# Turning undivided exponentials in the last attention stage, with two order tables made anew

## The chip, the cores and the metric

The kernel runs on one core of one Trainium2 chip. The metric is the device time of one execution, in microseconds. The core has five instruction streams, each executed in order: TensorE (PE; its weight loads are shown as PEld), VectorE (DVE), ScalarE (ACT), GpSimd (POOL) and SyncE (SP), which here only issues DMAs. They meet at semaphores alone.

## The reference

Four transformer blocks follow each other on x (batch 8, 128 tokens, width 256), with a context of the same shape.

```python
x = L0(x, ctx)   # 16 heads of 16: cross-attention to ctx, key mask; MLP 256-1024-256
x = L1(x, ctx)   # x attends to [ctx, x]; RMS norm; MLP
x = L2(x, ctx)   # twice: 16 heads of 128, cross-attention to ctx; MLP ("M2")
x = L3(x, ctx)   # "L3s" self-attention, "L3c" cross-attention, 16 heads of 16; MLP

# L3's attention
scores = einsum('bhqd,bhkd->bhqk', q, k) / sqrt(HD)
scores = scores * mask - 10000.0 * (1.0 - mask)
probs  = softmax(scores, axis=-1)
ctx    = einsum('bhqk,bhkd->bhqd', probs, v)     # v = ln_out @ w_v + b_v
x      = x + ctx @ w_o + b_o
```

## The kernel before

The program has three stages. **Stage A** (`ORDER_ONE`: L0 and L1) and **stage C** (`ORDER_TWO`: the MLP of L2, then L3s, L3c and their MLP) are lists of steps, one list for each engine, written out by hand: each engine runs its own steps in its list's order, and the semaphores make each step wait for what it reads and for the PSUM bank that it overwrites. A step's last number on PE is its PSUM bank. Between them stage B (the two attentions of L2) is a loop over 16 turns. The batch is cut into four streams `k` of two batch elements `b`.

In stage C attention runs in 16 **units** `n`, one for each layer (L3s, L3c), stream and batch element. A unit has 16 heads of 128 x 128 scores and is worked in two halves `r` of eight heads; half-unit `u = 2n + r` lives in `tiles[u % 4]` (128 x 1024 floats), so two units are under way at most. The steps of a unit, with the lines of the profile:

- `scores n`: PE multiplies into banks 0 to 3 (L842); DVE multiplies by the mask into the tile (L1191); POOL subtracts from the mask's offset (L1828).
- `minima n`: DVE takes each row's minimum (L1201); ACT takes the exponentials, head by head (`exp n r`, L1593).
- `even n r`: DVE sums the rows (L1206) and takes reciprocals (L1208); POOL multiplies the whole tile by them (L1834).
- `turn n r`: PE transposes the tile in two halves of four heads into banks 4 and 5 (L852), ACT copies them to `PT` (L1559).
- `weigh n`: PE multiplies `PT` with the values into bank 6 (L867); ACT adds the value bias and writes `OT` (L1508, `HEADS_ON["C"] = "ACT"`).
- `project n`: PE multiplies `OT` with the output weights (L881), DVE adds it and the pre-biased residual `xb` to x (L1222). POOL makes `xb` in `residual` (L1811).

The rest of stage C's lists are layer norms (DVE statistics, POOL `rstd` at L1747, ACT `xn`, PE transposes L717), projections (L730, L738, L794) and the MLPs (`up` L810, `down` L826).

Of the kernel before, what the change touches and what calls it, by code (L numbers as in the profile page):

```python
# [501 lines left out]
class Drains:  # L502
# [17 lines left out]
    ctx 0 0, turn_in L0 in 0 5, ctx 1 0, q L0 0 3, k L0 0 0 2, ctx 2 7, k L0 1 0 4, scores 0, k L0 2 0 7, ctx 3 5, v L0 2 0 4, scores 1,  # L520
    turn_in L0 in 3 5, v L0 3 0 7, turn_in L0 in 1 2, v L0 0 0 1, q L0 3 3, q L0 1 0, turn 0 0, scores 2, turn 0 1, turn_in L0 in 2 7, turn 1 0, weigh 0,
    scores 3, q L0 2 7, turn 1 1, k L0 3 0 1, project 0 4, weigh 1, v L0 1 0 3, turn 2 0, project 1 7, scores 4, turn 2 1, k L1 0 0 7, weigh 2, turn 3 0,
    turn_in L0 mlp 0 7, scores 5, turn 3 1, project 2 7, weigh 3, v L1 0 0 0, up L0 0 0 1, project 3 0, up L0 0 2 2, up L0 0 4 3, up L0 0 6 7, turn 4 0,
    scores 6, turn 4 1, down L0 0 0 7, down L0 0 1 0, turn_in L0 mlp 1 3, turn 5 0, weigh 4, scores 7, turn 5 1, project 4 7, turn_in L1 in 0 0, weigh 5,
    up L0 1 0 1, up L0 1 2 4, k L1 0 1 3, project 5 2, up L0 1 4 0, turn 6 0, q L1 0 1, up L0 1 6 7, scores 8, turn 6 1, k L1 1 0 7, down L0 1 0 1,
    turn_in L0 mlp 2 0, down L0 1 1 7, turn 7 0, turn_in L1 in 1 7, weigh 6, scores 9, turn 7 1, k L1 1 1 7, project 6 1, weigh 7, turn 8 0, v L1 0 1 7,
    scores 10, turn 8 1, project 7 7, v L1 1 0 0, q L1 1 1, up L0 2 0 3, up L0 2 2 2, up L0 2 4 7, turn 9 0, weigh 8, scores 11, turn 9 1, up L0 2 6 7,
    turn 10 0, weigh 9, down L0 2 0 7, scores 12, turn 10 1, k L1 2 0 7, turn 11 0, weigh 10, scores 13, turn 11 1, project 9 7, turn_in L0 mlp 3 4,
    weigh 11, down L0 2 1 3, v L1 1 1 2, up L0 3 0 4, up L0 3 2 7, project 11 2, turn 12 0, turn_in L1 in 2 7, turn 12 1, scores 14, weigh 12, turn 13 0,
    up L0 3 4 1, up L0 3 6 4, scores 15, turn 13 1, q L1 2 7, k L1 2 1 0, down L0 3 0 4, weigh 13, scores 16, turn 14 0, v L1 2 0 7, turn 14 1,  # L530
    down L0 3 1 1, v L1 2 1 2, project 13 5, turn_in L1 mlp 0 0, turn_in L1 in 3 2, turn 15 0, weigh 14, scores 17, turn 15 1, k L1 3 0 7, turn 16 0,
    weigh 15, scores 18, turn 16 1, up L1 0 0 7, project 15 0, up L1 0 2 3, up L1 0 4 1, up L1 0 6 2, turn 17 0, weigh 16, scores 19, turn 17 1,
    v L1 3 0 7, turn_in L1 mlp 1 0, k L1 3 1 3, down L1 0 0 1, q L1 3 2, turn 18 0, weigh 17, scores 20, turn 18 1, v L1 3 1 7, weigh 18, turn 19 0,
    scores 21, turn 19 1, down L1 0 1 7, project 17 0, up L1 1 0 1, up L1 1 2 2, up L1 1 4 7, turn 20 0, weigh 19, scores 22, turn 20 1, up L1 1 6 7,
    project 19 1, turn 21 0, weigh 20, scores 23, turn 21 1, down L1 1 0 7, turn_in L1 mlp 2 1, down L1 1 1 3, weigh 21, turn 22 0, up L1 2 0 0,
    turn 22 1, up L1 2 2 1, turn 23 0, weigh 22, up L1 2 4 7, turn 23 1, up L1 2 6 0, weigh 23, project 21 4, project 23 7, down L1 2 0 1, keys_of 0,
    turn_in L1 mlp 3 7, down L1 2 1 5, up L1 3 0 2, up L1 3 2 5, up L1 3 4 7, up L1 3 6 0, turn_in L1 out 1 4, turn_in L1 out 0 2, down L1 3 0 5,
    down L1 3 1 7, turn_in L1 out 2 3, keys_of 1, values_of 0, turn_in L1 out 3 7, queries_of 0, values_of 1, values_of 2,
    values_of 3, queries_of 1
""",  # L540
    "ACT": """
    wcut L0 k, ctx 0 0, turn_in L0 in 0 5, ctx 1 0, k L0 0 0 2, ctx 2 7, k L0 1 0 4, k L0 2 0 7, ctx 3 5, exp 0 0, exp 0 1, v L0 2 0 4, turn_in L0 in 3 5,
    v L0 3 0 7, turn_in L0 in 1 2, v L0 0 0 1, exp 1 0, turn 0 0, exp 1 1, turn 0 1, turn_in L0 in 2 7, exp 2 0, turn 1 0, exp 2 1, turn 1 1, k L0 3 0 1,
    exp 3 0, v L0 1 0 3, turn 2 0, exp 3 1, turn 2 1, k L1 0 0 7, turn 3 0, exp 4 0, turn 3 1, turn_in L0 mlp 0 7, exp 4 1, v L1 0 0 0, exp 5 0,
    up L0 0 0 1, up L0 0 2 2, up L0 0 4 3, turn 4 0, up L0 0 6 7, turn 4 1, exp 5 1, exp 6 0, exp 6 1, turn 5 0, turn_in L0 mlp 1 3, turn 5 1,
    turn_in L1 in 0 0, exp 7 0, up L0 1 0 1, up L0 1 2 4, k L1 0 1 3, up L0 1 4 0, turn 6 0, up L0 1 6 7, exp 7 1, k L1 1 0 7, exp 8 0, turn 6 1, exp 8 1,
    turn_in L0 mlp 2 0, turn_in L1 in 1 7, turn 7 0, turn 7 1, k L1 1 1 7, exp 9 0, turn 8 0, v L1 0 1 7, turn 8 1, exp 9 1, v L1 1 0 0, exp 10 0,
    exp 10 1, up L0 2 0 3, up L0 2 2 2, turn 9 0, up L0 2 4 7, turn 9 1, up L0 2 6 7, exp 11 0, exp 11 1, turn 10 0, turn 10 1, k L1 2 0 7, turn 11 0,
    turn 11 1, exp 12 0, exp 12 1, turn_in L0 mlp 3 4, exp 13 0, exp 13 1, v L1 1 1 2, up L0 3 0 4, up L0 3 2 7, turn 12 0, turn_in L1 in 2 7, turn 12 1,
    turn 13 0, up L0 3 4 1, up L0 3 6 4, exp 14 0, turn 13 1, exp 14 1, k L1 2 1 0, exp 15 0, exp 15 1, turn 14 0, v L1 2 0 7, turn 14 1, exp 16 0,  # L550
# [1711 lines left out]
```

## Time and profile before

| | us |
|---|---|
| median of 3 runs | 1029.7 |
| the 3 runs | 1029.73, 1029.70, 1028.91 |
| the profiled execution | 1029.54 |
| its span | 1028.3 |
| PE busy in the span | 997.2 |
| DVE, ACT, POOL busy | 789.0, 586.1, 712.5 |

The span runs from the first to the last recorded instruction; 1.24 us of the profiled execution lie around it. Busy time is the union of an engine's instructions. A matmul's record reaches from its start to the end of its drain, and so overlaps the next one's: in a stream of them the distance between starts, not the mean duration, is what one costs. Stage C begins at about 780 us. The granted TensorE clock stands as PEclk, 1.00 for 2.4 GHz.

### The profile page before, as it was taken

To read this page: it belongs to the slowest core of one execution; us is meant where nothing else is said; L and a number is where in the kernel's file an instruction comes from. 1 tells how busy PE (TensorE), PEld (TensorE's weight loads), DVE (VectorE), ACT (ScalarE), POOL (GpSimd) and SP (SyncE) were. 2 spreads that over 40 slices of the span, in tenths; PEclk is the share of its full clock that TensorE was granted. 3 is DMA by queue.
4 is the path that set the end of the run, shared out by engine and by line. 5 is a ranking of instruction groups with operands and counts; after the bars stand their busy time and mean duration, and the time that the engine had idled before them with its cause. 6 is when DMAs were issued, how large, how long until landed. Compare 5 with 4: busy or idle time off the path is not lost.

```text
span 1028.3 us, 21233 instructions
## 1 busy us (share of the span) xinstructions
PE 997.2 (97%) x8212; PEld 897.7 (87%) x8212; DVE 789.0 (77%) x1272; ACT 586.1 (57%) x1305; POOL 712.5 (69%) x659
## 2 busy tenths in 40 slices
PE   7899999999999999999999999999998999998998
PEld 7788878888889999999998999999997988777877
DVE  7997888998357778988868878888875488898761
ACT  5998888797535323233233333232335589999982
POOL 6895476755578888556368987756647488999961
PEclk9999999999999999999999999999999999999999
DMA  8200001000121220211120111110130000000000
GB/s 335 116 2 2 1 2 42 2 1 2 47 77 33 74 62 30 62 42 42 42 86 21 42 42 42 31 43 23 44 141 1 1 2 2 2 1 2 12 11 21
DMA packets 34219, 40.72 MB, mean 40 GB/s; under 512 B 2159, under 2 KB 31305, under 8 KB 32713
## 3 DMA queue, kind: packets, MB, share of 16 engines
q1 hardware_dynamic: 34121, 39.38, 11.6%
q8 instruction: 66, 1.08, 0.4%
q14 instruction: 32, 0.26, 0.1%
HBM read 38.32 MB, written 1.05 MB: 38 GB/s over the span
## 4 chain that ended last, share of the span: by engine, by line
PE 76%; POOL 11%; DVE 6%; ACT 4%; issue 2%; DMA 0%; SPq 0%; DVEq 0%; POOLq 0%; ACTq 0%
PE psum L946 10%; PE psum L810 9%; PE psum L826 9%; PE psum L964 7%; PE psum L1012 7%; PE psum L852 5%; PE psum L999 5%; PE psum L978 5%; PE psum L931 4%; PE psum L738 3%; PE psum L842 3%; PE psum L867 3%; PE psum L988 2%; POOL C tile L1828 2%; PE psum L881 2%
## 5 line engine op out<-in xcount | busy, mean ns | idle before, releaser
L1983 POOL TENSOR_TENSOR B tile<-B tile,B rec 128x1024 f32<-128x1024 f32 x32 | 61.0, 1912 | 101.9 <-DVE B rec L1369 101.9
L1834 POOL TENSOR_TENSOR A tile<-A tile,outer rec 128x1024 f32<-128x1024 f32 x48 | 91.0, 1905 | 57.8 <-DVE outer rec L1208 57.7
L1685 ACT COPY B PT<-psum 128x512 f32<-128x512 f32 x64 | 33.0, 600 | 138.0 <-PE psum L988 138.0
L1593 ACT ACTIVATE A tile<-A tile,outer min 128x128 f32<-128x128 f32 (+1 forms) x256 | 92.3, 448 | 2.6 <-DVE outer min L1201 2.5
L1593 ACT ACTIVATE C tile<-C tile,outer min 128x128 f32<-128x128 f32 x256 | 77.8, 401 | 1.1 <-DVE outer min L1201 1.0
L964 PE MATMUL psum<-B v hi,cT hi 128*128 128x256 f32 x256 | 71.9, 281 | 0.3 <-ACT B kT L1508 0.3
L964 PE MATMUL psum<-B v hi,cT lo 128*128 128x256 f32 x256 | 71.7, 280 | 0.0
L964 PE MATMUL psum<-B v lo,cT hi 128*128 128x256 f32 x256 | 71.7, 280 | 0.0
L1834 POOL TENSOR_TENSOR C tile<-C tile,outer rec 128x1024 f32<-128x1024 f32 x32 | 60.7, 1902 | 7.7 <-DVE outer rec L1208 7.7
L1194 DVE TENSOR_TENSOR A tile<-m,psum 128x1024 f32<-128x1024 f32 x48 | 56.5, 1216 | 9.1 <-PE psum L842 7.9
L1206 DVE TENSOR_REDUCE outer sum<-A tile 128x4 f32<-128x1024 f32 (+1 forms) x48 | 58.0, 1208 | 4.9 <-ACT A tile L1593 4.9
L1559 ACT COPY A PT<-psum 128x512 f32<-128x512 f32 x96 | 51.4, 590 | 18.1 <-PE psum L852 10.9
L999 PEld LDWEIGHTS psum<-B PT,B v 128*128 128x128 f32 x512 | 59.4, 192 | 1.1
L978 PE MATMUL psum<-B kT,B qT 128*128 128x128 f32 x512 | 59.8, 275 | 0.0
L999 PE MATMUL psum<-B PT,B v 128*128 128x128 f32 x512 | 59.8, 275 | 0.0
L978 PEld LDWEIGHTS psum<-B kT,B qT 128*128 128x128 f32 x512 | 58.5, 192 | 0.1
L826 PE MATMUL psum<-weights,C aT 128*128 128x256 f32 x256 | 57.2, 380 | 1.2 <-ACT C aT L1550 1.2
L826 PE MATMUL psum<-weights,A aT 128*128 128x256 f32 x256 | 57.8, 380 | 0.1
L852 PEld LDWEIGHTS psum<-ident,A tile 128*128 128x128 f32 x384 | 42.1, 141 | 18.2 <-issue 11.4
L1508 ACT ACTIVATE B OT0 hi<-psum,cols 128x512 fp32r<-128x512 f32 x32 | 21.9, 688 | 60.5 <-PE psum L999 60.4
L1201 DVE TENSOR_REDUCE outer min<-A tile 128x4 f32<-128x1024 f32 (+1 forms) x48 | 55.9, 1207 | 0.0
L826 PEld LDWEIGHTS psum<-weights,C aT 128*128 128x128 f32 x256 | 48.0, 190 | 7.8 <-issue 1.6
(358 smaller groups left out, 3550.6 us busy)
## 6 DMA issues: line engine op xcount, KB each, us to landing
raw<-in_wq SPq DMA_DIRECT2D x32, 128.0 KB, 2.9
raw<-in_wk SPq DMA_DIRECT2D x32, 128.0 KB, 3.0
raw<-in_wv SPq DMA_DIRECT2D x16, 256.0 KB, 2.8
raw<-in_wo SPq DMA_DIRECT2D x16, 256.0 KB, 2.7
weights<-in_weights_c SPq DMA_DIRECT2D x4, 1024.0 KB, 6.0
weights<-in_weights_a SPq DMA_DIRECT2D x1, 3072.0 KB, 21.5
weights<-in_weights_a SPq DMA_DIRECT2D x1, 2048.0 KB, 12.4
wide<-in_bias_v SPq DMA_DIRECT2D x2, 1024.0 KB, 10.1
```

The source lines that it names most:

```text
L810: i = pe.matmul(bank(z)[:, n * T:(n + 1) * T], w[wp][:, c, n * P:(n + 1) * P], h[hp][:, c, :], start=(c, wp, hp) == (0, 0, 0), stop=c == C ...
L826: i = pe.matmul(bank(z)[:, 0:D], part.aT(k)[:, c, b * P:(b + 1) * P], w2[:, c, :], start=c == 0, stop=c == FC - 1)
L852: i = pe.transpose(bank(4 + half)[:, j * P:(j + 1) * P], part.tiles[u % 4][:, q * P:(q + 1) * P], m.ident[:, :])
L946: i = pe.matmul(bank(z + n), m.block(kind, wt, wp), m.half_of(kind, src, sp), start=(wp, sp) == (0, 0), stop=wp == 1)
L964: i = pe.matmul(bank(z)[:, k * 2 * HK:(k + 1) * 2 * HK], m.bcT[cp][:, c, (2 * n + k) * S:(2 * n + k + 1) * S], m.cut["v"][wp][:, c, :], st ...
L978: i = pe.matmul(bank(z + b // 4)[:, (b % 4) * S:(b % 4 + 1) * S], m.qT[h][:, b * S:(b + 1) * S], m.kT[h][:, b * S:(b + 1) * S], start=True ...
L999: i = pe.matmul(bank(z)[:, k * P:(k + 1) * P], m.vv[:, 4 * n + k, h * HK:(h + 1) * HK], m.bPT[:, h, n, k * P:(k + 1) * P], start=True, sto ...
L1012: i = pe.matmul(bank(z)[:, k * D:(k + 1) * D], m.bOT[h][op][:, (2 * n + k) * S:(2 * n + k + 1) * S], m.cut["o"][wp][:, h, :], start=(h, op ...
L1206: dve.tensor_reduce(part.sum[:, u % 4, 0:ly.per], tile(u, ly.nk), AX.X, ALU.add).then_inc(s["sum_made"].sem, s["sum_made"].mark((st, u)))
L1593: i = act.activation(of_head, of_head, ACT.Exp, bias=part.min[:, u % 4, h:h + 1], scale=-1.0)
L1834: pool.tensor_tensor(tile(u, ly.nk), tile(u, ly.nk), part.rec[:, u % 4, 0:ly.per].unsqueeze(2).to_broadcast([P, ly.per, ly.nk]), ALU.mult) ...
L1983: pool.tensor_tensor(tv, tv, m.brec[:, h, :].unsqueeze(2).to_broadcast([P, B, S]), ALU.mult).then_inc(s["normalised"].sem, s["normalised"] ...
```

## The change

**Lists.** Both tables of steps are new for all four engines. Stage A's has the same steps in another order. Stage C's has one step more, `rows`, and `weigh` is added to the lists of engines that did not have it.

**Undivided exponentials (stage C only).** `turn` on PE no longer waits for `evened`, the division on POOL, but for `exp_made`. `even n r` on POOL no longer touches the 128 x 1024 tile: it spreads the 8 reciprocals of each row to 128 x 64 twice (each reciprocal repeated for the 16 columns of its head) into a new buffer `rec_rows`. At the end of `weigh n` PE waits for both of them and transposes `rec_rows` (two 128 x 128) into the second half of bank 6. ACT copies these 128 x 256 back to `rec_rows`, and DVE multiplies the weighed heads in bank 6 by them into `OT`, in one instruction, where ACT had written `OT` in two. The heads of stage C thus move from ACT to DVE.

**Bias.** Since the value bias is no longer added to the heads, the step `rows` multiplies it once with the output weights of L3s and L3c on PE, and DVE adds the two rows to the output biases; `residual` of L3's attentions waits for that.

```diff
-HEADS_ON = {"A": "DVE", "C": "ACT"}
+HEADS_ON = {"A": "DVE", "C": "DVE"}
...
+            self.Cs.rec_rows = sc("C rec rows", [P, 2, C, P])
...
         def turn(n, r):
-            pe.wait_ge(s["evened"].sem, s["evened"].at((st, u)))
+            ready = "exp_made" if st == "C" else "evened"
+            pe.wait_ge(s[ready].sem, s[ready].at((st, u)))
...
# weigh, PE, behind the 16 matmuls of the unit
+            if st == "C":
+                pe.wait_ge(s["evened"].sem, s["evened"].at((st, 2 * n + 1)))
+                for c in range(C):
+                    i = pe.transpose(bank(6)[:, (C + c) * P:(C + c + 1) * P], part.rec_rows[:, n % 2, c, :], m.ident[:, :])
+        def rows(z):
+            once("w_late_loaded", 32)
+            claim(z, "rows_made", "rows")
+            for n, name in enumerate(("L3s", "L3c")):
+                for c in range(C):
+                    i = pe.matmul(bank(z)[:, n * D:(n + 1) * D], layers[name].bv[:, c:c + 1].to_broadcast([P, P]), layers[name].wo[:, c, :],
+                                  start=c == 0, stop=c == C - 1)
...
# reciprocal, DVE
+            if st == "C" and n >= 2:
+                dve.wait_ge(s["evened"].sem, s["evened"].at((st, u - 4)))
# heads, DVE
+            if st == "C":
+                dve.wait_ge(s["rec_copied"].sem, s["rec_copied"].at(("C", n)))
+                dve.tensor_tensor(part.OT[b][:, :, :], bank(6)[:, 0:C * P].rearrange("p (c q) -> p c q", c=C), part.rec_rows[:, n % 2, :, :], ALU.mult).then_inc(
+                    s["heads_drained"].sem, s["heads_drained"].mark((ly.name, k, b)))
+                return
...
# weigh, ACT
+            elif what == "weigh" and st == "C":
+                act.wait_ge(s["weighed"].sem, s["weighed"].at((st, a[0])))
+                act.copy(part.rec_rows[:, a[0] % 2, :, :], bank(6)[:, C * P:2 * C * P].rearrange("p (c q) -> p c q", c=C)).then_inc(
+                    s["rec_copied"].sem, s["rec_copied"].mark((st, a[0])))
...
# even, POOL
+            if st == "C":
+                if n >= 2:
+                    pool.wait_ge(s["heads_drained"].sem, s["heads_drained"].at((units[n - 2][0].name, *units[n - 2][1:3])))
+                for c in range(C):
+                    i = pool.tensor_copy(part.rec_rows[:, n % 2, c, r * 4 * HD:(r + 1) * 4 * HD].rearrange("p (j q d) -> p j q d", j=2, q=2),
+                                         part.rec[:, u % 4, :].rearrange("p (j c q) -> p j c q", j=2, c=C)[:, :, c, :].unsqueeze(3).to_broadcast([P, 2, 2, HD]))
+                i.then_inc(s["evened"].sem, s["evened"].mark((st, u)))
+                return
...
# the lists, stage C, PE, the first line of each
-    output 0, output 1, output 2, turn_in M2 mlp 0 7, output 3, turn_in M2 mlp 1 1, up M2 0 0 4, up M2 0 2 5, up M2 0 4 1, up M2 0 6 2,
+    output 0, output 1, output 2, output 3, turn_in M2 mlp 0 4, rows 2, up M2 0 0 2, up M2 0 2 4, up M2 0 4 7, up M2 0 6 2, turn_in M2 mlp 1 1,
```

Three places of stage C show what moves. The first is POOL from the mask work of unit 6 (a row with `wide`, L3c's mask, x2) to that of unit 9; `outer rec` are the reciprocals. Before:

```order
L1828 TENSOR_TENSOR C tile<-wide,C tile 128x1024 x2
L1834 TENSOR_TENSOR C tile<-C tile,outer rec 128x1024
L1747 TENSOR_TENSOR outer rstd<-outer ve,half 128x2
L1828 TENSOR_TENSOR C tile<-wide,C tile 128x1024 x2
L1834 TENSOR_TENSOR C tile<-C tile,outer rec 128x1024
L1811 TENSOR_TENSOR raw<-x_all,rows 128x512
L1834 TENSOR_TENSOR C tile<-C tile,outer rec 128x1024 x2
L1828 TENSOR_TENSOR C tile<-wide,C tile 128x1024 x2
L1834 TENSOR_TENSOR C tile<-C tile,outer rec 128x1024
L1817 TENSOR_TENSOR C h lo<-C xn,C h hi 128x512
L1828 TENSOR_TENSOR C tile<-wide,C tile 128x1024 x2
L1834 TENSOR_TENSOR C tile<-C tile,outer rec 128x1024
```

and with the change, where `C rec rows` is the new buffer and `x2` or `x4` counts instructions, two to a half-unit:

```order
L1865 TENSOR_TENSOR C tile<-wide,C tile 128x1024 x2
L1875 COPY C rec rows<-outer rec 128x64 x4
L1865 TENSOR_TENSOR C tile<-wide,C tile 128x1024 x2
L1782 TENSOR_TENSOR outer rstd<-outer ve,half 128x2
L1848 TENSOR_TENSOR raw<-x_all,rows 128x512
L1875 COPY C rec rows<-outer rec 128x64 x4
L1865 TENSOR_TENSOR C tile<-wide,C tile 128x1024 x2
L1875 COPY C rec rows<-outer rec 128x64 x2
L1854 TENSOR_TENSOR C h lo<-C xn,C h hi 128x512
L1782 TENSOR_TENSOR outer rstd<-outer ve,half 128x2
L1875 COPY C rec rows<-outer rec 128x64 x2
L1865 TENSOR_TENSOR C tile<-wide,C tile 128x1024 x2
```

Each division of a 128 x 1024 tile between the pairs of mask work has become two copies of 128 x 64. The second place is PE from `weigh 4` on, behind the keys of L3c's stream 2 (`C tile` are the exponentials, `C PT` their turned copy). Before:

```order
L867 MATMUL psum<-C PT,C vaug 32x128 x16
L717 MATMUL psum<-ident,C xn 128x128 x4
L852 MATMUL psum<-ident,C tile 128x128 x8
L842 MATMUL psum<-C kT,C qT 128x256 x8
L852 MATMUL psum<-ident,C tile 128x128 x8
L881 MATMUL psum<-weights,C OT 128x256 x2
```

and with the change:

```order
L871 MATMUL psum<-C PT,C vaug 32x128 x16
L877 MATMUL psum<-ident,C rec rows 128x128 x2
L856 MATMUL psum<-ident,C tile 128x128 x16
L845 MATMUL psum<-C kT,C qT 128x256 x8
L871 MATMUL psum<-C PT,C vaug 32x128 x16
L877 MATMUL psum<-ident,C rec rows 128x128 x2
L856 MATMUL psum<-ident,C tile 128x128 x8
L720 MATMUL psum<-ident,C xn 128x128 x4
```

Each weighing is now followed by two transposes of `rec rows`, and `weigh 5` now comes right behind the scores of unit 7; behind the transposes stand the turns and scores of later units. The third place is DVE, from the last sum of unit 5 to those of unit 6 (`OT` are the heads). Before:

```order
L1206 TENSOR_REDUCE outer sum<-C tile 128x8
L1208 RECIPROCAL outer rec<-outer sum 128x8
L1201 TENSOR_REDUCE outer min<-C tile 128x8 x2
L1191 TENSOR_TENSOR C tile<-psum,wide 128x1024 x2
L1206 TENSOR_REDUCE outer sum<-C tile 128x8
L1208 RECIPROCAL outer rec<-outer sum 128x8
L1239 TENSOR_SCALAR outer nb<-outer mv,outer rstd 128x1 x2
L1222 TENSOR_TENSOR x_all<-psum,raw 128x256
L1201 TENSOR_REDUCE outer min<-C tile 128x8 x2
L1206 TENSOR_REDUCE outer sum<-C tile 128x8
```

and with the change, from the minima of unit 6 on:

```order
L1220 TENSOR_REDUCE outer min<-C tile 128x8 x2
L1236 TENSOR_TENSOR C OT<-psum,C rec rows 128x256
L1210 TENSOR_TENSOR C tile<-psum,wide 128x1024 x2
L1225 TENSOR_REDUCE outer sum<-C tile 128x8
L1229 RECIPROCAL outer rec<-outer sum 128x8
L1225 TENSOR_REDUCE outer sum<-C tile 128x8
L1229 RECIPROCAL outer rec<-outer sum 128x8
L1236 TENSOR_TENSOR C OT<-psum,C rec rows 128x256
L1220 TENSOR_REDUCE outer min<-C tile 128x8 x2
L1265 TENSOR_SCALAR outer nb<-outer mv,outer rstd 128x1 x2
L1248 TENSOR_TENSOR x_all<-psum,raw 128x256
```

The heads' multiplication is a new row between the minima of one unit and the masking of another; sums and reciprocals keep their number.

## Rows read from the trace of the kernel before

**Rows 1.** Busy shares of the whole span, from the page (40 slices).

```profile
PE 997.2 (97%) x8212; PEld 897.7 (87%) x8212; DVE 789.0 (77%) x1272; ACT 586.1 (57%) x1305; POOL 712.5 (69%) x659
...
PE   7899999999999999999999999999998999998998
```

**Rows 2.** Busy time by stage, from the windows (columns in the first row).

```profile
core 0: us, PE busy (x) PEld busy (x) DVE busy (x) ACT busy (x) POOL busy (x), PEclk, DMA share, GB/s
0.00:60.00 60.00, 50.01 (x468) 42.32 (x469) 52.86 (x110) 47.20 (x125) 47.70 (x50) 1.00 0.50 193
60.00:260.00 200.00, 199.31 (x1947) 170.42 (x1947) 175.53 (x282) 169.56 (x377) 122.02 (x86) 1.00 0.02 7
260.00:780.00 520.00, 517.98 (x3740) 483.32 (x3739) 390.91 (x554) 172.23 (x291) 360.76 (x416) 1.00 0.16 51
780.00:820.00 40.00, 36.15 (x285) 33.31 (x284) 17.73 (x56) 20.89 (x44) 17.20 (x16) 1.00 0.00 1
820.00:880.00 60.00, 58.53 (x521) 51.13 (x520) 49.22 (x85) 55.50 (x148) 53.39 (x31) 1.00 0.01 2
880.00:940.00 60.00, 53.24 (x555) 44.66 (x554) 54.69 (x96) 56.82 (x163) 55.59 (x32) 0.94 0.01 2
940.00:990.00 50.00, 48.48 (x444) 42.60 (x442) 39.97 (x71) 48.19 (x130) 45.39 (x26) 1.00 0.02 7
990.00:1028.30 38.30, 33.50 (x264) 29.95 (x264) 8.07 (x24) 15.75 (x34) 10.42 (x9) 1.00 0.06 21
...
820.00:990.00 170.00, 160.25 (x1516) 138.40 (x1514) 143.88 (x250) 160.50 (x437) 154.37 (x87) 0.98 0.01 3
```

**Rows 3.** Chain of waits, 903 to 943: start us, us, what.

```profile
903.54 1.90 POOL C tile L1834
905.44 4.73 POOL C tile L1828 x2
910.16 1.87 POOL C tile L1834
...
912.08 1.69 PE psum L852 x8
...
922.91 1.90 POOL C tile L1834
...
942.28 0.87 PE psum L852 x8
```

**Rows 4.** Waits, 880 to 940: who waited for whom, us, times, longest.

```profile
PEld psum L852 <- POOL C tile L1834: 5.5, 5, 1.6
PE psum L852 <- POOL C tile L1834: 3.5, 5, 1.2
DVE C tile L1191 <- PE psum L852: 3.3, 3, 1.5
```

**Rows 5.** Last stage, instructions by line and form (busy us, mean ns, idle before).

```profile
L1593 ACT ACTIVATE C tile<-C tile,outer min 128x128 f32<-128x128 f32 x256 | 77.8, 401 | 1.1 <-DVE outer min L1201 1.0
L1834 POOL TENSOR_TENSOR C tile<-C tile,outer rec 128x1024 f32<-128x1024 f32 x32 | 60.7, 1902 | 7.7 <-DVE outer rec L1208 7.7
...
L1206 DVE TENSOR_REDUCE outer sum<-C tile 128x8 f32<-128x1024 f32 x32 | 38.7, 1208 | 4.3 <-ACT C tile L1593 4.0
L1828 POOL TENSOR_TENSOR C tile<-ms,C tile 128x1024 f32<-128x1024 f32 x16 | 38.2, 2410 | 9.2 <-DVE C tile L1191 9.2
...
L1508 ACT ACTIVATE C kT<-psum,bk_parity,parity 128x256 f32<-128x256 f32 x28 | 13.6, 577 | 1.4 <-PE psum L738 1.3
...
L1508 ACT ACTIVATE C OT<-psum,cols 128x128 f32<-128x128 f32 x32 | 10.0, 366 | 2.9 <-PE psum L867 2.8
...
L1222 DVE TENSOR_TENSOR x_all<-psum,raw 128x256 f32<-128x256 f32 x16 | 6.5, 411 | 2.7 <-PE psum L881 2.7
```

**Rows 6.** POOL's small instructions, from the groups by line (whole span, then to 300).

```profile
L1882 POOL CAST B k hi<-raw 128x256 fp32r<-128x256 f32 x8 | 3.2, 396 | 0.0
...
L1751 POOL TENSOR_SCALAR outer nb<-outer mv,outer rstd 128x1 f32<-128x1 f32 x8 | 2.0, 265 | 0.2
L2010 POOL MEMSET A vaug<- 128x1024 f32 x2 | 1.8, 952 | 0.0
```

**Rows 7.** TensorE in the last stage, in order of time: start, duration.

```profile
887.77 1.04 PE L852 MATMUL psum<-ident,C tile 128*128 128x128 f32 x8
889.81 1.15 PE L842 MATMUL psum<-C kT,C qT 32*128 32x256 f32 x16 [1.00 <-issue]
891.77 1.84 PE L852 MATMUL psum<-ident,C tile 128*128 128x128 f32 x8 [0.82 <-POOL C tile L1834]
```

**Rows 8.** The last units: POOL's divisions, then TensorE, in order of time.

```profile
987.20 3.75 POOL L1834 TENSOR_TENSOR C tile<-C tile,outer rec 128x1024 f32<-128x1024 f32 x2 [0.84 <-DVE outer rec L1208]
...
991.58 1.90 POOL L1834 TENSOR_TENSOR C tile<-C tile,outer rec 128x1024 f32<-128x1024 f32 x1
...
992.96 1.09 PE L852 MATMUL psum<-ident,C tile 128*128 128x128 f32 x8
...
998.20 1.13 PE L881 MATMUL psum<-weights,C OT 128*128 128x256 f32 x4 [0.75 <-ACT C OT L1508]
```

**Rows 9.** TensorE's waits to 270 by releaser (us, times, longest).

```profile
PE psum L852 <- POOL A tile L1834: 2.1, 2, 1.4
PE psum L717 <- DVE A xn L1159: 2.1, 1, 2.1
PE psum L723 <- POOL ident L2001: 1.7, 1, 1.7
```

**Rows 10.** DMA issues from 735 to 800 (count, KB, us to landing); digits in 40 slices.

```profile
DMA  0000079504899940000000000000000000000000
...
weights<-in_weights_c SPq DMA_DIRECT2D x3, 1024.0 KB, 5.3
weights<-in_weights_c SPq DMA_DIRECT2D x3, 256.0 KB, 6.0
```

More of the change, by code:

```diff
@@ L519 @@
     "PE": """
[L520 to L539, printed above, removed]
+    ctx 0 2, turn_in L0 in 0 7, ctx 1 4, q L0 0 0, k L0 0 0 1, k L0 1 0 4, ctx 2 5, turn_in L0 in 1 7, scores 0, k L0 2 0 5, v L0 0 0 4, ctx 3 7,
@@ L543 @@
[L543 to L550, printed above, removed]
@@ L574 @@
-    even 23 1, stats L1 out 1, stats L1 out 0, weigh 23, project 21 4, project 23 7, stats L1 mlp 3, down L1 2 0 1, turn_in L1 mlp 3 7, down L1 2 1 5,
-    stats L1 out 2, down L1 3 0 5, parts 0, down L1 3 1 7, stats L1 out 3, parts 1, parts 2, parts 3, values_of 0, values_of 1, values_of 2,
-    values_of 3, queries_of 1
+    stats L0 in 0, xn L0 in 0, ctx 0 2, wcut L0 k, ctx 1 4, stats L0 in 1, q L0 0 0, stats L0 in 2, stats L0 in 3, ctx 2 5, scores 0, minima 0,
+    ctx 3 7, scores 1, even 0 0, minima 1, even 0 1, q L0 1 0, q L0 3 7, even 1 0, scores 2, minima 2, even 1 1, q L0 2 5, even 2 0, weigh 0,
@@ new lines @@
+    even 15 0, minima 16, even 15 1, down L0 3 1 4, turn_in L1 mlp 0 1, turn_in L1 in 3 7, project 13 3, even 16 0, even 16 1, scores 17, minima 17,
+    scores 18, weigh 15, even 17 0, even 17 1, project 15 3, stats L1 mlp 1, minima 18, scores 19, minima 19, even 18 0, even 18 1, down L1 0 0 2,
+    turn_in L1 mlp 1 0, q L1 3 3, even 19 0, even 19 1, weigh 17, scores 20, minima 20, scores 21, minima 21, down L1 0 1 7, stats L1 out 0,
+    project 17 0, even 20 0, even 20 1, even 21 0, even 21 1, weigh 19, scores 22, project 19 0, stats L1 mlp 2, minima 22, scores 23, even 22 0,
@@ L577 @@
+    minima 23, even 22 1, turn_in L1 mlp 2 1, down L1 1 0 7, down L1 1 1 2, even 23 0, even 23 1, weigh 21, stats L1 out 1, weigh 23, project 21 4,
+    project 23 0, stats L1 mlp 3, down L1 2 0 4, turn_in L1 mlp 3 1, down L1 2 1 4, stats L1 out 2, down L1 3 0 4, parts 0, parts 1, down L1 3 1 1,
+    stats L1 out 3, parts 2, parts 3, values_of 0, values_of 1, values_of 2, values_of 3, queries_of 1
 """,
     "POOL": """
[L579 removed]
@@ L907, in do @@
                 project(*a)
+            elif what == "rows":
+                rows(*a)
             elif what == "keys_of":
@@ L1275, in do @@
                 output(2, NP_ - 1, a[0])
+            elif what == "rows":
+                at = ROWS.index("L3_b_ao")
+                dve.wait_ge(s["rows_projected"].sem, s["rows_projected"].at("rows"))
+                dve.tensor_tensor(m.rows[:, at:at + 2, :], m.rows[:, at:at + 2, :], bank(a[0]).rearrange("p (n d) -> p n d", n=2), ALU.add).then_inc(
+                    s["rows_made"].sem, s["rows_made"].mark("rows"))
         return do
```

200 lines of the change are left out of this document (113 added, 87 removed).

## The prediction

> **What bounds the kernel now.** The page's busy line and PE's slices come first [rows 1]: PE is busy 97% of the span, so most of it can only be shortened by less work for PE. The windows say where PE is not full [rows 2]. From 60 to 780 us it is busy 717.3 of 720 us; nothing is won there. It is idle 10.0 us in the first 60, 3.9 from 780 to 820, 9.8 from 820 to 990 and 4.8 in the last 38.3. The change works in stage C, from 780 on, where 18.4 us are idle, and there the stretch from 820 to 990, which holds nearly all of the units, decides: of 170 us PE is busy 160.3, ACT 160.5, POOL 154.4 and DVE 143.9. All four are near full, and none runs through. From 880 to 940 it is worst: PE 53.2 of 60, ACT 56.8, POOL 55.6, DVE 54.7.
>
> The chain of waits tells which of them the others wait for [rows 3]. It runs on POOL: a division of 1.90, two mask subtractions of 4.73, a division of 1.87, and then PE's transposes, again and again. The waits agree [rows 4]: in those 60 us PE and its weight loads wait for the division five times each, 5.5 us on the loads' account (both accounts describe the same waits), and DVE's masking then waits 3.3 us for the transposes, since they free the tile. The granted clock belongs to it. It was 0.94 there, and the two levels can be seen in one operation: eight transposes take 1.04 us at 887.77 and 1.84 at 891.77, at 1.2 GHz, after PE had stood 1.00 and 0.82 us shortly before [rows 7]. A clock of 0.94 over 60 us is 3.6 us of PE's speed.
>
> **POOL.** The 32 divisions go, 60.7 us [rows 5]. In their place come 64 copies of 128 x 64, which no row shows. The small ones near them are 0.27 us for 128 x 1 and 0.40 for 128 x 256 [rows 6]; I take 0.27, being nearer in size to the first, 17 us (bounds 17 and 26). POOL goes from 154 to about 111 us in the stretch. It stops being a limit in either case, so this price does not reach the sum.
>
> **The path of a unit.** Before, a half-unit's transposes waited, behind the exponentials, for sum (1.21), reciprocal (0.20) and division (1.90), 3.3 us in all, with POOL's mask work often ahead of the division [rows 3, 5]. Now they wait for the exponentials alone. A tile's round from masking to masking is shorter by these 3.3 us or more; since four tiles serve two units, that is what lets the engines run closer to full.
>
> **ACT.** Two heads' instructions of a unit, 10.0 / 16 = 0.63 us, become one copy of 128 x 256 out of PSUM; the nearest row is the keys' 13.6 / 28 = 0.49 [rows 5]. 16 x 0.14 = 2.2 us go: ACT has 158.3 us left in the stretch. The exponentials, 77.8 us, stay.
>
> **DVE.** It takes the 16 multiplications of the heads. The nearest row also adds a 128 x 256 operand to PSUM, 0.41 us [rows 5]: 6.5 us, so 150.4 in the stretch. `rows` adds one of 128 x 512, under 1 us, before 820, where DVE is busy 17.7 of 40 us [rows 2].
>
> The rows show for a read of 128 x 256 from PSUM 0.49 us on ACT and 0.41 on DVE [rows 5]. The Trainium skill (VectorE: DVE Perf Modes, Specifications) states that VectorE sits closer to SBUF and ScalarE closer to PSUM, which speaks against moving heads to DVE. If DVE needed ACT's old 0.63 for them, it would have 154.0 us, and still less than ACT; the trace does not agree, and the sum goes by the rows.
>
> **PE.** Transposes of `rec rows`: 32, at 0.87 / 8 = 0.11 us [rows 3], 3.5 us. `rows` adds four products of 128 x 256 with single-precision weights; `project` has two of them, recorded as four, in about 1.13 us [rows 8], so 2.3 us with the last drain. They stand between 780 and 820, where PE is idle 3.9 us and waits for the first layer norm; I take 0 (bounds 0 and +2.3). The late weights, for which `rows` waits, are no obstacle: the transfers end in the fifteenth slice of 735 to 800, by 760 [rows 10]. In the stretch PE's 160.3 holds the slow clock's 3.6; without it and with the 3.5 it is 160.2.
>
> **The waits that are new.** `weigh` ends in a wait for POOL's copies, and whatever PE's list has behind it waits too. From the exponentials it takes 1.21 + 0.20 + 2 x 0.27 = 1.95 us if DVE and POOL are free; PE in that time has the second turn (0.87), ACT's copy of it and the weighing itself (about 1), so it should be hidden, with little to spare. The heads then need PE, ACT (0.49) and DVE (0.41), where ACT alone had 0.63: 0.3 us later, and bank 6 is freed that much later. A unit takes about 10 us, so I take 0 for both; the bound is the third rival.
>
> **The sum.** In the stretch ACT is now the fullest with 158.3, PE has 160.2. Before, ACT was busy 94.4% of it. With a shorter path and three full engines in place of four I take 96%: 158.3 / 0.96 = 165, so -5 us (PE is then 97% busy; it reaches 99.7% from 60 to 260). Bounds: 94.4% as before gives 167.7, -2.3; PE at 99.7% gives 160.7, -9.3. At the end, the last exponentials are followed by a division until 993.5 and by the last projection at 998.20 [rows 8]; without it the last turn can come up to 3.5 us earlier, of which PE's other work leaves some 2: -2 (bounds 0 and -3.5). From there to the end stand the two last streams' MLP products, unchanged. Stage A has the same work in another order. Its first 60 us wait 1.7 and 2.1 us for the first data and 2.1 for divisions [rows 9], and behind 60 PE is 99.7% busy, so the order can win 2 us at most; I take 0 (bounds -2 and +2). Sum: 1029.54 - 5 - 2 = 1022.5 us for the profiled execution; the median of the runs shown is 0.16 above it, which changes nothing.
>
> **The rivals.**
> First, less: the order of waits holds the engines at the share they had, -2.3 in the stretch and nothing at the end. For it: DVE is worst off from 880 to 940, where 54.7 + 2.5 (six units) = 57.2 of 60 us are needed, so only 2.8 can go there. Against: it has 49.2 of 60 before, and the lists are free to shift. 1027.2.
> Second, more: PE becomes the bound and runs through, -9.3 - 3.5 and -1 in stage A: 1015.7. For it: POOL's share falls by 44 us. Against: ACT would have to be 98.5% busy.
> Third, slower: PE stands in `weigh`. DVE puts the sum of the second half behind other work (a masking pair is 2 x 1.22), POOL its copies behind a mask pair (4.73), and PE, which before could not be held by a late reciprocal once it had turned, waits with scores and turns queued behind. One DVE instruction of 1.21 us at half of the units costs 9.7, against the 7 won: 1032.2. It decides from 7 / 16 = 0.44 us a unit on. Against it: in the lists the second half's sum comes right behind the masking of the next unit, and PE's weighing only after that unit's scores.
> Fourth, the change does not do what it says, PE waiting for the reciprocals as before: the waits on L852 are replaced by equal ones behind L867, with 3.5 us more of PE work. 1033; it shares the third's place and I count them together.
>
> **How the numbers follow.** Forecast 1022.5, from 1018.5 to 1026.5 with the bounds of its terms: 0.57. Less: 0.16. More: 0.14. Slower: 0.13. A measurement of this kernel can tell about 0.2%, 2.1 us, from no change. Faster by that is the forecast, more, and somewhat over a third of less: 0.77; the rest of less and a little of slower, 0.12; slower 0.11. The range from 1016 to 1031 leaves out the far part of more and most of slower.
>
> **What would show it.** Right: no wait of L852 for POOL in stage C, POOL near 70% from 820, the clock at 1.00 from 880 to 940, ACT over 95% busy until its last exponentials, these ending some 5 us earlier, and the last projection some 7. The heads' multiplication at 0.41 and the copies at 0.27. Wrong: waits of the transposes of `rec rows` for POOL that add up to more than 7 us (slower), DVE's share above ACT's with ACT waiting for minima (less), or PE idle in stage A that was not there.

## The result and the profile after

The changed kernel takes 1022.71 us (median of 4 runs, 1022.61 to 1022.81) beside 1029.72 us of the kernel before on the same chip (4 runs, 1028.91 to 1031.95): ratio 0.9939, 95% interval [0.9926, 0.9953]. It is 0.6% faster. The forecast was 1022.5 us. The profiled execution took 1022.81 us with a span of 1021.6, before 1029.54 and 1028.3.

The page's busy line of the changed kernel, whole span (compare [rows 1]):

```profile
PE 998.7 (98%) x8252; PEld 899.9 (88%) x8252; DVE 796.9 (78%) x1289; ACT 582.1 (57%) x1289; POOL 664.0 (65%) x691
```

The windows of the changed kernel by stage, columns as in [rows 2]. The stretch of the units is taken to 985 here: ScalarE runs 422 instructions in it; from 820 to 990 it ran 437 before [rows 2], and the change takes 16 off it.

```profile
0.00:60.00 60.00, 50.80 (x475) 42.87 (x475) 53.70 (x107) 45.49 (x118) 45.89 (x48) 1.00 0.50 193
...
780.00:820.00 40.00, 37.26 (x285) 33.93 (x284) 18.16 (x54) 20.74 (x44) 17.34 (x14) 1.00 0.00 1
820.00:880.00 60.00, 59.81 (x532) 53.20 (x531) 50.84 (x94) 55.34 (x149) 38.27 (x38) 1.00 0.01 1
880.00:940.00 60.00, 55.35 (x600) 45.96 (x599) 58.98 (x101) 59.23 (x167) 43.65 (x50) 1.00 0.01 2
...
820.00:985.00 165.00, 160.17 (x1559) 138.61 (x1561) 146.53 (x263) 156.57 (x422) 108.43 (x117) 1.00 0.01 3
```

POOL is no longer near full: 43.7 of 60 us from 880 to 940, where it had 55.6. DVE and ACT take its place there with 59.0 and 59.2 of 60. The clock is 1.00 where it was 0.94.

Its last stage by line and form, 780 to 1022 (columns as in [rows 5]): the new instructions, and the sum that stands on the path.

```profile
L1225 DVE TENSOR_REDUCE outer sum<-C tile 128x8 f32<-128x1024 f32 x32 | 38.5, 1204 | 1.8 <-ACT C tile L1624 1.7
...
L1875 POOL COPY C rec rows<-outer rec 128x64 f32<-128x64 f32 x64 | 12.5, 243 | 6.1 <-DVE outer rec L1229 6.1
...
L877 PE MATMUL psum<-ident,C rec rows 128*128 128x128 f32 x32 | 7.0, 300 | 0.0
L1236 DVE TENSOR_TENSOR C OT<-psum,C rec rows 128x256 f32<-128x256 f32 x16 | 6.6, 412 | 4.3 <-ACT C rec rows L1660 4.2
L1660 ACT COPY C rec rows<-psum 128x256 f32<-128x256 f32 x16 | 6.0, 376 | 3.0 <-PE psum L877 3.0
```

And its chain of waits from 885, start us, us, what (compare [rows 3], which ran on POOL's divisions and masks):

```profile
888.76 2.52 ACT C tile L1624 x9
...
893.69 0.96 ACT C PT L1590 x2
...
896.53 2.35 ACT C tile L1624 x8
898.87 0.98 ACT C xn L1539 x2
899.86 1.81 ACT C kT L1539 x4
901.67 2.23 ACT C tile L1624 x8
```

ACT runs from instruction to instruction here. No POOL piece stands in the chain from 885 to 910.

**Where the 6.7 us of the span went.** Read from the order of TensorE's work in both traces: the middle stage's first matmul comes at 267.7 instead of 269.2 us (-1.5). From there to the first unit's scores it is 545.2 us instead of 543.9 (+1.3). From these to unit 15's scores 159.0 instead of 164.2 (-5.2). From there to the end 49.7 instead of 51.1 (-1.4). So the units give most, and two terms that the forecast took as 0, the first stage and the front of the last one, nearly cancel. The profiled execution of before was one whose clock fell; what that is worth stands in the last section.

### The profile page after: what moved, and what is told of

It is laid out like the page before. It is cut to its first block, busy times and chain, and to the rows that moved or that the text cites. A ratio compares the mean times of both kernels' runs of the same rounds, so it can differ in the third digit from the quotient of the medians.

```text
span 1021.6 us, 21422 instructions
## 1 busy us (share of the span) xinstructions
PE 998.7 (98%) x8252; PEld 899.9 (88%) x8252; DVE 796.9 (78%) x1289; ACT 582.1 (57%) x1289; POOL 664.0 (65%) x691
## 4 chain that ended last, share of the span: by engine, by line
PE 84%; ACT 6%; DVE 5%; POOL 3%; issue 1%; DMA 1%; SPq 0%; POOLq 0%; DVEq 0%; ACTq 0%
PE psum L829 11%; PE psum L965 10%; PE psum L1031 8%; PE psum L983 8%; PE psum L813 8%; PE psum L856 6%; PE psum L1018 5%; PE psum L997 5%; PE psum L950 4%; PE psum L845 3%; PE psum L741 3%; PE psum L871 3%; PE psum L1007 3%; PE psum L898 2%; PE psum L797 2%; ACT C tile L1624 2%
## 5 line engine op out<-in xcount | busy, mean ns | idle before, releaser
L829 PE MATMUL psum<-weights,C aT 128*128 128x256 f32 x256 | 57.2, 380 | 0.3 <-ACT C aT L1581 0.2
L856 PEld LDWEIGHTS psum<-ident,A tile 128*128 128x128 f32 x384 | 42.2, 141 | 17.0 <-issue 12.5
L829 PEld LDWEIGHTS psum<-weights,A aT 128*128 128x128 f32 x256 | 47.7, 190 | 7.1 <-issue 1.1
```

What stands on the lines that cost most here:

```text
L829: i = pe.matmul(bank(z)[:, 0:D], part.aT(k)[:, c, b * P:(b + 1) * P], w2[:, c, :], start=c == 0, stop=c == FC - 1)
L856: i = pe.transpose(bank(4 + half)[:, j * P:(j + 1) * P], part.tiles[u % 4][:, q * P:(q + 1) * P], m.ident[:, :])
```

## The experiments

Each ran beside the kernel before on one chip, in three groups; before had 1029.14, 1029.21 and 1028.07 us in them, and 1028.26, 1027.97 and 1027.97 in its executions at a mean granted clock of 1.000. So times of different groups are compared here to some 0.3 us and no closer. The changed kernel ran once more in the first group only. The two kernels without `rows` or without its addition leave the last layer's two value biases out of the sums.

**The anchor**, no edit.

> The changed kernel once more, as the anchor of the kernels that run beside it. Both theories: 1022.7 us, within 0.3 us, ratio to the kernel before 0.993.

Measured 1022.73 us (1022.37 to 1024.5, 5 runs), ratio 0.9943 [0.9931, 0.9955].

**The first stage's list alone** (the kernel before; `ORDER_ONE`, all engines, from the changed one).

```diff
 ORDER_ONE = {
     "PE": """
-    ctx 0 0, turn_in L0 in 0 5, ctx 1 0, q L0 0 3, k L0 0 0 2, ctx 2 7, k L0 1 0 4, scores 0, k L0 2 0 7, ctx 3 5, v L0 2 0 4, scores 1,
+    ctx 0 2, turn_in L0 in 0 7, ctx 1 4, q L0 0 0, k L0 0 0 1, k L0 1 0 4, ctx 2 5, turn_in L0 in 1 7, scores 0, k L0 2 0 5, v L0 0 0 4, ctx 3 7,
...
```

> The kernel before, with only the first outer stage's list of steps made anew; the last stage is as before in its list and its operations. Theory (the two traces' milestones are the cause): the middle stage's first matmul comes at 267.7 instead of 269.2 us and nothing gives that back, so the time is 1.5 us lower, 1028.2 us, ratio 0.9985. Rival 1, the prediction's own step (the list of the first stage is worth nothing): 1029.7 us, ratio 1.000. Rival 2 (what the first stage gains is lost at the middle stage's first transfers): the middle stage starts earlier and its waits for loads grow by as much, ratio 1.000.

Measured 1026.97 us (12 runs), ratio 0.9982 [0.9971, 0.9994]. The middle stage's first matmul is at 267.3, and from it to the first unit's scores it is 544.0 us, as before. The theory's side: the list is worth about 2 us, and nothing later takes it back.

**The last stage's change alone** (the changed kernel with before's `ORDER_ONE`).

> The changed kernel with the first outer stage's list of steps as before; all of the last stage's change is in. Theory: 7.0 us less 1.5 us of the first stage, so 1024.2 us, ratio 0.9947, and with the kernel that has only the first list the two parts add up to the whole. Rival (the parts are not independent, or the first list is worth nothing): 1022.7 us, ratio 0.993.

Measured 1025.23 us (1024.93 to 1025.47), ratio 0.9965 [0.9952, 0.9978]. The two parts' ratios multiply to 0.9947, the whole is 0.9943: they add up. The theory's size was too large for this part, 3.9 us by the medians instead of 5.5, and 3.0 against the executions of before at a clock of 1.000. Its trace has the changed kernel's lengths: 545.4 us to the first unit's scores, 159.1 to unit 15's, 49.7 to the end. So the loss at the front belongs to this part and is already off its gain.

**Without `rows`** (its step taken out of TensorE's and VectorE's lists, and POOL's wait for it).

```diff
-    ... turn_in M2 mlp 0 4, rows 2, up M2 0 0 2, ...
+    ... turn_in M2 mlp 0 4, up M2 0 0 2, ...
```

> The changed kernel without the step that projects the value biases of the last layer into rows and adds them to the row that every token's sum takes; those two value biases are left out of the sums. Theory: the step's 2 us of matmuls on TensorE and the 0.7 us behind them on VectorE, which stand ahead of the first up projections of the last stage, cost 1.3 to 2 us there (the first unit's scores come at 812.9 in the changed kernel though the middle stage ended 1.5 us earlier), and nothing gives it back: 1021.2 us, 1.5 us below the changed kernel. Rival, the prediction's own term (the step lies beside the wait for the first normalised tokens and costs nothing): 1022.7 us.

Measured 1022.71 us (1022.24 to 1023.56), no gain. My theory falls; the prediction's 0 stands. TensorE in that kernel, in order of time, start, duration:

```profile
781.13 0.66 PE L691 MATMUL psum<-ident,C xn 128*128 128x128 f32 x4
784.87 0.38 PE L784 MATMUL psum<-C h hi,rows hi 128*128 128x256 f32 x1 [3.09 <-POOL C h lo L1823]
785.09 0.28 PE L784 MATMUL psum<-C h lo,rows hi 128*128 128x256 f32 x1
...
786.43 0.41 PE L784 MATMUL psum<-C h hi,weights lo 128*128 128x256 f32 x1
```

and in the changed one:

```profile
781.25 0.66 PE L720 MATMUL psum<-ident,C xn 128*128 128x128 f32 x4
781.94 1.96 PE L885 MATMUL psum<-weights,cols 128*128 128x256 f32 x8
785.00 0.38 PE L813 MATMUL psum<-C h hi,rows hi 128*128 128x256 f32 x1 [1.10 <-POOL C h lo L1854]
```

The 1.96 us of matmuls lie in a hole of 3.1 us in which POOL makes the low half. Without them TensorE stands still all that time, and about 1 us after it has started again each up matmul takes 0.41 instead of 0.28 us: the clock has fallen. The windows of that kernel around it (columns as in [rows 2]):

```profile
775.00:785.00 10.00, 6.77 (x53) 6.37 (x54) 7.63 (x29) 3.40 (x6) 7.86 (x12) 1.00 0.01 2
785.00:795.00 10.00, 9.85 (x64) 9.46 (x65) 3.44 (x14) 7.33 (x15) 2.69 (x4) 0.83 0.01 2
```

So the gain could have been lost to the clock. That asked for another run.

**The matmuls kept, the addition left out** (only VectorE's `rows 2` and the waits for it go).

> The changed kernel with the eight matmuls that project the two value biases left where they are on TensorE, and only VectorE's addition behind them left out (so those biases are missing in the sums, as in the kernel without the whole step). That kernel had the same time as the changed one, and its profile shows TensorE idle for 3.1 us ahead of the first up projections and the granted clock at 0.83 in the 10 us behind. Theory (the matmuls lie in a hole and cost nothing, and without them the longer hole costs the clock what the missing addition gives): the clock is 1.00 again in 785 to 795, and the time is 0.7 to 1.5 us below the changed kernel, 1021.2 to 1022.0 us. Rival (the addition is worth nothing either, the gelus' place in ScalarE's list holds the front): 1022.7 us, clock 1.00.

Measured 1023.10 us (1022.25 to 1023.88), ratio 0.9948 [0.9936, 0.996]. Clock 1.00 (785 to 795), and no gain: the rival. From the middle stage's first matmul to the first unit's scores it is 545.2 us in the changed kernel, 545.1 without `rows`, 545.0 here. Neither the matmuls, nor the addition, nor some 3 us at the lower clock set the front.

**The front's order on two engines.**

```diff
 "PE":
-    turn_in M2 mlp 0 4, rows 2, up M2 0 0 2,
+    turn_in M2 mlp 0 4, rows 5, up M2 0 0 2,
 "DVE":
-    output 3, rows 2, xn M2 mlp 1, stats M2 mlp 2,
+    output 3, xn M2 mlp 1, stats M2 mlp 2, rows 5,
 "ACT":
-    xn M2 mlp 1, xn M2 mlp 2, up M2 0 0 2, up M2 0 2 4,
+    xn M2 mlp 1, up M2 0 0 2, up M2 0 2 4, xn M2 mlp 2,
```

> The changed kernel with two moves at the last stage's front: VectorE adds the projected rows behind the statistics of the third slice instead of ahead of the second slice's shift (in another bank, 5), and ScalarE normalises the third slice after the second pair of the first slice's gelus instead of ahead of them. TensorE's list is as it was but for the bank. Theory: the 1.4 us in which TensorE stands still at 789 to 791 us, waiting for gelus to free a bank, go, the first unit's scores come 1.2 us earlier, and the time is 1021.5 us. Rival 1 (the third slice's transposes are late in turn): no gain, 1022.7 us. Rival 2 (the clock falls behind a longer hole elsewhere): 1023 to 1024 us.

Measured 1021.09 us (1020.92 to 1021.20), ratio 0.9923 [0.9907, 0.9939]; faster than both kernels. The move of `rows` alone, without ScalarE's:

> The changed kernel with one of the two moves of the kernel that took 1021.09 us: VectorE adds the projected rows behind the third slice's statistics (in bank 5); ScalarE's list is as it was. Theory (the addition stands ahead of the second slice's shift by 0.7 us, and the gelus wait behind the two normalisations on ScalarE): the move alone gives half of it, 1021.9 us. Rival 1 (the addition's place is the whole of it): 1021.1 us. Rival 2 (ScalarE's order is the whole of it): 1022.7 us.

Measured 1022.42 us (1022.36 to 1024.71), front 545.0 us: within 0.3 us of the changed kernel. The front is ScalarE's order, 543.7 us with it mended as well. In the changed kernel ScalarE normalises two slices, the second late, before it loads its table and turns to the first gelus, and TensorE stands still 1.45 us for them:

```profile
784.91 1.09 ACT L1539 ACTIVATE C xn<-x_all,outer nb,outer rstd 128x256 f32<-128x256 f32 x2 [1.31 <-DVE outer nb L1265]
787.40 1.09 ACT L1539 ACTIVATE C xn<-x_all,outer nb,outer rstd 128x256 f32<-128x256 f32 x2 [1.40 <-DVE outer nb L1265]
788.51 1.28 ACT L1581 ACT_TABLE_LOAD   x1
789.81 2.30 ACT L1581 ACTIVATE C aT<-psum,cols 128x256 f32<-128x256 f32 x6
...
790.79 0.35 PE L813 MATMUL psum<-C h hi,C fc1 hi 128*128 128x256 f32 x1 [1.45 <-ACT C aT L1581]
```

With the second normalisation moved, the table comes while ScalarE waits for TensorE anyway:

```profile
783.51 1.09 ACT L1497 ACTIVATE C xn<-x_all,outer nb,outer rstd 128x256 f32<-128x256 f32 x2 [0.22 <-DVE outer nb L1223]
784.62 1.28 ACT L1539 ACT_TABLE_LOAD   x1
786.40 0.84 ACT L1539 ACTIVATE C aT<-psum,cols 128x256 f32<-128x256 f32 x2 [0.50 <-PE psum L771]
```

**A small division in the old list.** POOL divides only 8 of each head's 128 columns in the last stage; the rest stays undivided, and all waits stay.

```diff
+            nk = ly.nk if st == "A" else 8
-            pool.tensor_tensor(tile(u, ly.nk), tile(u, ly.nk), ...
+            pool.tensor_tensor(tile(u, ly.nk)[:, :, 0:nk], tile(u, ly.nk)[:, :, 0:nk], ...
```

> The kernel before, both lists as they were, in which GpSimd divides only 8 of the columns of each head in the last stage (128 partitions x 32 or 64 elements instead of 1024), so that the division left out is most of it and its heads are mostly undivided. All waits stay. Theory A (what the change won in the stretch of the units is GpSimd's division on the way from the exponentials to the transposes): the instruction falls from 1.85 to about 0.3 us, the waits of the weights' transposes for it (3.5 us in 820 to 990) go, and the stage is 3 to 5 us shorter, 1025 to 1026 us beside 1029.1. Theory B (the gain is the new list, which stands turn ahead of reciprocal; with the old list every engine is held at the same places): within 1 us of the kernel before, 1028 to 1029 us.

Measured 1027.16 us (1026.03 to 1035.10, 10 runs), ratio 0.9994 [0.9976, 1.0011]. The executions at a clock of 1.00 have a median of 1026.7 beside 1028.0 of before: 1.3 us. POOL's line in its last stage:

```profile
L1835 POOL TENSOR_TENSOR C tile<-C tile,outer rec 128x64 f32<-128x64 f32 x32 | 9.5, 297 | 27.4 <-DVE outer rec L1208 27.4
```

The division went from 1.90 to 0.30 us and 51 us of POOL's work went, yet the time hardly moved. (That profile is of an execution whose clock stood at 0.95 up to 850 us, so no time of TensorE is taken from it.) The measurement falls between A and B, nearer to B, and the interval of all runs has 1, no change, within it. The waits of the transposes' loads for POOL from 820 to 998 went down from 8.1 us in ten, not away, and ScalarE is what fills up:

```profile
PEld psum L852 <- POOL C tile L1835: 2.1, 3, 1.2
...
880.00:940.00 60.00, 54.40 (x558) 45.42 (x556) 55.25 (x96) 59.43 (x169) 39.90 (x31) 0.97 0.01 2
```

ScalarE has in this kernel the heads that the change takes from it. The sum, the reciprocal and POOL's queue still stood between exponentials and transposes, so half of the 3.3 us of path stayed; what that half would give in the old list is open.

**POOL's load put back, off the transposes' path.**

```diff
+                for again in range(5):
+                    if again:
+                        i.then_inc(s["spent"].sem, ...)
+                        pool.wait_ge(s["spent"].sem, ...)
                 for c in range(C):
                     i = pool.tensor_copy(part.rec_rows[...], part.rec[...])
```

> The changed kernel with GpSimd's two copies of reciprocals per half unit made five times instead of once, each pair waiting for the pair before, so GpSimd carries 8 more copies of about 0.25 us per half unit (62 us over the stage), as much as the division took, and the weighing's transposes wait for it while the turning doesn't. Theory (GpSimd's load is not what bounds; only the wait between exponentials and transposes was): 1022.7 to 1024.5 us. Rival (GpSimd's throughput bounded the stage before, by what queues behind the division: the additions of masks and the low halves): the whole gain of the units goes, 1027 to 1028 us.

Measured 1058.94 us (1057.6 to 1059.26), ratio 1.0288 [1.027, 1.0307]: 36 us slower than the changed kernel, far beyond both. Its chain of waits from 900 to 960:

```profile
917.38 2.39 POOL C tile L1865
...
920.17 0.42 POOL C rec rows L1879 x2
920.65 0.42 POOL C rec rows L1879 x2
921.12 0.41 POOL C rec rows L1879 x2
922.01 1.24 POOL C h lo L1854
923.24 0.66 POOL outer rstd L1782
924.32 0.42 POOL C rec rows L1879 x2
```

and two of its waits from 820 to 990:

```profile
DVE outer min L1220 <- POOL C tile L1865: 14.7, 14, 2.0
...
PE psum L877 <- POOL C rec rows L1879: 4.8, 3, 2.5
```

From 917 on the chain is nearly all POOL again; in the whole stretch from 900 to 960 two thirds of it are. POOL carries 65.1 us of these copies, where it had 12.5. Its list is worked off in order, so the copies hold up the mask subtractions, low halves and statistics behind them, and `weigh` on TensorE (L877) is held too. The last is the third rival's mechanism; the changed kernel has it at 0.2 us in 820 to 990, since its copies are short. The clock is 0.91 from 880 to 940 there. The edit delays `weigh` as well as loading POOL, so how the 36 us divide between load, delay and clock is open. What it shows is that the new list needs a POOL that is quick.

**One more copy on ScalarE; one more multiplication on VectorE.** Both repeat the unit's instruction and wait for its first.

```diff
+                act.copy(part.rec_rows[...], bank(6)[...]).then_inc(s["spent"].sem, ...)
+                act.wait_ge(s["spent"].sem, ...)
```

> The changed kernel with ScalarE's copy of the turned reciprocals made twice per unit, the second waiting for the first: 16 times 0.38 us and as many short waits, about 7 us more on ScalarE, of which 14 fall into 820 to 990. Theory (ScalarE, 95% busy there, sets the pace): 4 to 7 us longer, 1027 to 1030 us. Rival (TensorE, 97% busy there, sets it and ScalarE has room): under 2 us longer, 1023 to 1024.7 us.

Measured 1026.54 us (10 runs), ratio 0.9975 [0.9963, 0.9987], 3.8 us over the changed kernel for 16 x 0.37 = 6.0 us of work.

```diff
+                dve.tensor_tensor(part.OT[b][...], bank(6)[...], part.rec_rows[...], ALU.mult).then_inc(s["spent"].sem, ...)
+                dve.wait_ge(s["spent"].sem, ...)
```

> The changed kernel with VectorE's multiplication of the heads by the reciprocals made twice per unit, the second waiting for the first: 16 times 0.41 us and as many short waits, about 7.5 us more on VectorE. ScalarE's copy made twice (16 times 0.38 us) gave 3.8 us longer, 0.6 us for each us of the work added. Theory (VectorE, 98% busy in 880 to 940, sets the pace there as much as ScalarE, the two handing over to each other): 3 to 5 us longer, 1026 to 1028 us. Rival (VectorE has room, 88% busy over 820 to 990): under 1.5 us longer, 1023 to 1024 us.

Measured 1026.35 us (11 runs), ratio 0.9983 [0.9974, 0.9992], 3.6 us for 16 x 0.42 = 6.8 us of work. The second is in its theory's range, the first just under its own: 0.6 and 0.5 us for each us added, a difference that the groups can't resolve. The two share the pace. One reading of the change falls with that, that it won by taking work off ScalarE: 4.0 us less there and 6.6 more on VectorE would, at these prices, cost about 1 us (an estimate from the two runs), so what the units won would have to come from elsewhere.

**The copy on VectorE instead of ScalarE**, on the front with both moves.

```diff
-                act.copy(part.rec_rows[...], bank(6)[...])
+                dve.tensor_copy(part.rec_rows[...], bank(6)[...])
```

> The kernel that took 1021.09 us (the two moves at the last stage's front) with the copy of the turned reciprocals on VectorE instead of ScalarE, right ahead of the multiplication: 6.0 us leave ScalarE, some 6.6 us and 16 short waits come on VectorE, and the multiplication no longer waits for another engine. Theory (both engines pace the units alike, 0.6 us for each us of work): no gain or up to 1.5 us longer, 1021 to 1022.6 us. Rival 1 (ScalarE alone sets the pace): 3 us shorter, 1018 us. Rival 2 (VectorE's 98% in 880 to 940 decides): 3 us or more longer, 1024 us.

Measured 1023.33 us (1023.28 to 1023.86), ratio 0.9952 [0.9939, 0.9964]: 2.2 us over the 1021.09 without it, which ran in another group; by the ratios to before, which hold its executions at a fallen clock too, it is 3.0. That is 0.7 us beyond the theory's range and between it and rival 2. From 880 to 940 in that kernel:

```profile
880.00:940.00 60.00, 53.62 (x583) 44.47 (x576) 59.15 (x105) 56.05 (x154) 41.74 (x48) 1.00 0.01 2
```

VectorE stays at 59 of 60 us, TensorE falls from 55.4 to 53.6 and ScalarE from 59.2 to 56.1. In that stretch VectorE is the one that can take nothing. The prices of the two runs before, 0.6 for ScalarE and 0.5 for VectorE, would have given next to no change, so they do not simply add.

**Not tried.** The old division under the new list: TensorE's turn would wait there for a reciprocal that stands, on VectorE, behind work that needs later steps of TensorE. The list's share and the method's share of the last stage can't be separated from that side. Nor was ScalarE's move at the front made alone.

## Why the prediction was right

**POOL.** Forecast 111 us in 820 to 990, 0.27 us a copy. Measured 0.243 a copy and 108.4 in 820 to 985. As predicted, POOL is no limit any more: from 903 to 943, where the chain ran on it [rows 3], it now runs on ScalarE, VectorE and TensorE, with no piece of POOL.

**The path of a unit.** The waits of the weights' transposes for POOL [rows 4] are gone; the most that L856 waits for another engine in 880 to 940 is 1.3 us in three waits, for ScalarE's copy. The units' scores 5.2 us shorter, 5 forecast for the stretch. But the step's reason, the shorter path with the lists free to follow, is shown only in part: 1.6 of the 3.3 us of path and 51 us of POOL's work taken out in the old list gave 1.3 us at full clock, the whole change of the stage 3.0, or about 4.3 without its loss at the front. How much of the difference is the rest of the path and how much the list stays open. And some 1.6 of the 5.2 us, by the executions in the last section, is the clock, which the forecast had inside its share and not as a term. The new list then stakes the time on POOL being quick (36 us when it isn't).

**ACT.** The copy took 0.376 us, not 0.49, so 4.0 us went instead of 2.2. The stretch came to about 165 us all the same, counted by ScalarE's instructions, with ACT at 94.9% of it (156.6), not 96: a work term too large and a share too high made up for each other. DVE, which filled up beside ACT, is the likely reason that the share stayed; that was not tested by itself. The prediction's own signs came out smaller than it wrote them: the last exponentials end at 985.8 instead of 989.5, 3.7 us earlier and not 5, the last projection starts 5.5 us earlier and not 7, and POOL is at 66%.

**DVE.** 0.412 us for the heads, 0.41 forecast; the row gave the right price. The Trainium skill (VectorE: DVE Perf Modes, Specifications) has ScalarE closer to PSUM and VectorE closer to SBUF. The prediction wrote that the trace does not agree, but compared unlike instructions: a plain copy of 128x256 out of PSUM took 0.376 us on ScalarE here and 0.407 on VectorE in the run with the copy moved, so the traces agree, by 0.03 us. What the prediction had weighed too lightly is the place: 57.2 of 60 us was its estimate for 880 to 940 (in the first rival); measured 59.0. The doubled multiplication shows what a us more on DVE costs, 0.5.

**PE.** A pair of transposes of `rec rows` holds TensorE 0.27 us until the next matmul starts (885.37 to 885.64), so 4.3 us, against 3.5. `rows`: 0, with bounds 0 to 2.3. It is 0: two kernels without it show no gain. The clock at 1.00 from 880 to 940 came as written.

**New waits.** Taken as 0. The transposes of `rec rows` wait for POOL 0.2 us in 820 to 990. What comes behind the heads costs about 1 us: TensorE waits for them once 0.6 us ahead of L871 and once 0.5 ahead of L898. The slower rival's mechanism is a real one (the loaded POOL shows it), but in the changed kernel it costs next to nothing.

**The end and the first stage.** -2 forecast at the end, -1.4 measured from unit 15's scores on, but -3.1 from the last exponentials on, where the forecast had its border. Units and end together are 6.6 us shorter, 7 forecast. Stage A: 0 taken, bound -2; the middle stage starts 1.5 us earlier in the changed kernel's trace and 1.9 in that of the first list alone, which is worth 2.2 us by the medians. Behind 60 us TensorE was 99.7% busy before and 99.8 after; the gain is 0.8 us ahead of 60 and the rest ahead of 269.

**Missing from the sum.** The front of the last stage, +1.3. The sum looked for its cost at `rows`, where it isn't: ScalarE's list was moved too, and a normalisation put ahead of the gelus, which no term priced. With the first stage's -1.5 it cancels, so the total of -7 met 6.7 of the span by more luck than its terms show.

## What to carry to other kernels

Where four engines hand tiles round, taking work off one of them may pay only in part while the order on the others stays: here most of POOL's division left out in the old order gave 1.3 us, and all of it off the path, in a new order, 3.0. That the order makes the difference is likely and not shown, since the two also differ in how much of the path went; test the two apart before crediting either. Price what a new list moves on every engine, the ones without new instructions too: the one loss of this change was a normalisation in front of a gelu. And before crediting or blaming a step beside a hole, ask which engine ends last there: here work that fitted into the hole was free, and so was a slow clock.
